# Moving a quarter of the conditioned weight deltas to GpSimd, with |h| written to a PSUM bank

## What is computed

```
scale = cond @ norm_w.T + 1.0
h = x * (scale[:, None, :] * rsqrt(mean(x * x) + EPS))
val, gate = split(h @ up_w.T)                  # 512 -> 2 x 2048
h = val * gelu(gate)
y = act_quant(h) @ weight_quant(down_w).T + x  # act_quant: one max |h| per row
# second layer, on y
dWd = ((h_lang @ Wdd.T + bdd) * 0.1).reshape(B, 128, 512)
dWu = ((h_lang @ Wdu.T + bdu) * 0.1).reshape(B, 512, 128)
out = y + relu(y @ (Wd + dWd) + bd) @ (Wu + dWu) + bu
```

## Time and profile before

| quantity | value |
|---|---|
| median of three runs | 942.75 us |
| the profiled execution | 943.0 us, its span 941.2 us |
| TensorE (PE) busy | 933.6 us, 99% |
| VectorE (DVE) busy | 675.3 us, 72% |
| ScalarE (ACT) busy | 437.6 us, 46% |
| GpSimd (POOL) busy | 53.4 us, 6% |
| granted TensorE clock | full in all 40 slices |

### The profile page before, as it was taken

One profiled execution on the slowest core, in us unless ns is written; L12 is line 12 of the kernel. 1 busy time (PEld: TensorE's weight loads), 2 busy tenths in 40 slices (PEclk: granted clock), 3 DMA queues, 4 the chain that ended last, 5 costly groups with the idle time before them and its releaser, 6 DMA issues.

```text
span 941.2 us, 13789 instructions
## 1 busy us (share of the span) xinstructions
PE 933.6 (99%) x5266; PEld 464.4 (49%) x5266; DVE 675.3 (72%) x1030; ACT 437.6 (46%) x800; POOL 53.4 (6%) x53
## 2 busy tenths in 40 slices
PE   8999999999999999999999999999999999999998
PEld 6555544444444444444444444444444444455586
DVE  5778888766877696767877687757877685256766
ACT  6898677224731276214742166213742255214443
POOL 1000000000000000000000000000000000000564
PEclk9999999999999999999999999999999999999999
DMA  8899654564346543664347543664347534421584
GB/s 286 239 219 217 169 151 131 150 193 137 101 140 170 161 134 112 159 168 155 112 131 177 152 138 99 173 174 146 110 127 186 149 90 135 112 68 35 185 307 179
DMA packets 118810, 145.36 MB, mean 154 GB/s; under 512 B 51796, under 2 KB 57432, under 8 KB 118232
## 3 DMA queue, kind: packets, MB, share of 16 engines
q1 hardware_dynamic: 118744, 144.48, 53.2%
HBM read 112.72 MB, written 20.97 MB: 142 GB/s over the span
## 4 chain that ended last, share of the span: by engine, by line
PE 97%; ACT 1%; DMA 1%; DVE 0%; issue 0%; SPq 0%; DVEq 0%; ACTq 0%
PE bank L1088 23%; PE bank L1090 23%; PE bank L1089 23%; PE bank L1190 10%; PE bank L1147 6%; PE bank L1200 1%; PE bank L1327 1%; PE bank L1336 1%; PE bank L1068 1%; PE bank L1349 1%; PE bank L1357 1%; PE bank L1359 1%; PE bank L1358 1%; PE bank L1366 1%; DMA xn<-in_x 1%; PE bank L1367 1%
## 5 line engine op out<-in xcount | busy, mean ns | idle before, releaser
L1088 PE MATMUL bank<-x_split,w_hi 128*128 128x512 f16 x1016 | 385.4, 379 | 0.0
L1089 PE MATMUL bank<-x_split,w_hi 128*128 128x512 f16 x1016 | 385.2, 379 | 0.0
L1090 PE MATMUL bank<-x_split,w_lo 128*128 128x512 f16 x1016 | 385.2, 379 | 0.0
L829 DVE STREAM_TRANSPOSE delta_reg<-delta_reg 128x512 f32<-128x512 f32 x256 | 262.4, 1108 | 51.7 <-DMA delta_reg<-in_L_cond_Wdu 19.3
L643 ACT ACTIVATE g<-h 128x512 f32<-128x512 f32 x128 | 80.6, 630 | 301.6 <-DVE h L925 301.6
L1090 PEld LDWEIGHTS bank<-x_split,w_lo 128*128 128x128 f16 x1016 | 99.4, 98 | 120.0
L1088 PEld LDWEIGHTS bank<-x_split,w_hi 128*128 128x128 f16 x1016 | 99.4, 98 | 119.2 <-issue 6.6
L1089 PEld LDWEIGHTS bank<-x_split,w_hi 128*128 128x128 f16 x1016 | 99.4, 98 | 113.2
L925 DVE SCALAR_TENSOR_TENSOR h<-bank,desc,g 128x512 f32<-128x512 f32 x128 | 93.1, 727 | 81.7 <-issue 57.9
L627 ACT ACTIVATE g<-bank,desc 128x512 f32<-128x512 f32 x128 | 87.5, 683 | 118.1 <-PE bank L1090 117.9
L1190 PE MATMUL bank<-wqT,qreg 128*128 128x512 fp8e4 x448 | 101.3, 379 | 0.0
(11 more groups left out here) (175 smaller groups left out, 628.6 us busy)
## 6 DMA issues: line engine op xcount, KB each, us to landing
delta_reg<-in_L_cond_Wdd SPq DMA_DIRECT2D x128, 256.0 KB, 2.9
delta_reg<-in_L_cond_Wdu SPq DMA_DIRECT2D x128, 256.0 KB, 2.9
qreg<-in_L_cond_up_w SPq DMA_DIRECT2D x32, 256.0 KB, 4.7
xr<-in_x SPq DMA_DIRECT2D x30, 256.0 KB, 3.8
x_scratch<-xr SPq DMA_DIRECT2D x30, 256.0 KB, 3.2
xn<-in_x SPq DMA_DIRECT2D x7, 1024.0 KB, 5.7
h<-in_L_cond_down_w SPq DMA_DIRECT2D x4, 1024.0 KB, 7.3
delta_reg<-in_L_cond_down_w SPq DMA_DIRECT2D x8, 512.0 KB, 4.6
```

The costliest lines, as they stand in the source:

```text
L829: dve.transpose(natT[:, t, k, :, :].rearrange("p a (r e) -> p e a r", e=4), nat[:, v % HALVES, :]).then_inc(nat_turned, 1)
L1088: pe.matmul(bank[:, :], w_hi[:, k, cols], xh[:, par, k, :], start=(k == 0), stop=False)
L1089: pe.matmul(bank[:, :], w_hi[:, k, cols], xl[:, par, k, :], start=False, stop=False)
L1090: mm = pe.matmul(bank[:, :], w_lo[:, k, cols], xh[:, par, k, :], start=False, stop=(k == KD - 1))
```

## The change

There are now 96 units on the old path, batched by four instead of eight, so that TensorE has 24 batches of 16 matmuls instead of 16 batches of 32 (a batch was 32 matmuls in the program, 64 in the trace, since each fp32 product is recorded twice). The remaining quarter of the delta rows, half of Wdu, is cut into 64 parts of 256 KB. SyncE loads a part into one of two places. GpSimd multiplies it by the four condition vectors (four instructions of 512 columns) and adds halves together twice (two of 512 and two of 256 columns), with waits on its own results between; VectorE sums the remaining 32 columns (`sum_part`, 64 of them, one in each slot of `sum_slots`) and later adds the result to the up weights (`up_weights`). GpSimd may be at most two parts ahead of VectorE's sums.

|h| is now written by ScalarE into the VAL bank that the value was in; VectorE's maximum reads it there, and TensorE's next value products into that bank wait for the maximum instead of for h. The scales are no longer copied by ScalarE to SBUF; VectorE multiplies by them out of PSUM bank TB. `s_bc` now holds the four condition vectors.

`load_deltas` now has 32 DMAs of 32 or 64 KB instead of 8 of 128 KB and 16 of 64 KB, and `turn_delta_up` has two transposes instead of four.

```diff
-    GROUPS = 16
-    UNITS, HALVES, NATT = 128, 3, 8
+    GROUPS = 12
+    UNITS, HALVES, NATT = 96, 3, 4
+    PARTS = 64
...
+        part_w = delta_reg[:, 11:13, :].rearrange("p s (d h) -> p s d h", d=4)
+        part_mul = delta_reg[:, 13:15, :].rearrange("p b (d h) -> p b d h", d=4)
+        part_low = delta_reg[:, 15:17, :].rearrange("p s (b d h) -> p s b d h", b=NB, d=4)
+        part_sum = delta_reg[:, 17:19, :].rearrange("p s e -> p (s e)").rearrange("p (b d) -> p b d", b=NB)
+        cond_all = s_bc[:, :].rearrange("p (b h) -> p b h", b=NB)
...
+        def abs_tile(c, j):
+            return g[:, j % 2, :] if is_last(c) and j >= FT - 2 else VAL[j % 2][:, :]
...
+        unit_slots, free_from = {}, 13
+        for n in range(FT * NCH):
+            long_slot = n >= FT and 9 <= n % FT < 13
+            while free_from <= n and sum(map(len, unit_slots.values())) < UNITS and len(unit_slots.get(n, [])) < 1 + long_slot:
+                u = sum(map(len, unit_slots.values()))
+                unit_slots.setdefault(n, []).append(u)
+                if u % NATT == NATT - 1:
+                    free_from = n + 2
+
         def units_at(c, j):
-            if is_first(c):
-                return [j - 13] if j >= 13 else []
-            if c == NCH - 1:
-                return [UNITS - 5 + j] if j < 5 else []
-            u = 3 + 20 * (c - 1) + j + min(max(j - 9, 0), 4)
-            return [u, u + 1] if 9 <= j < 13 else [u]
+            return unit_slots.get(FT * c + j, [])
 
         def batch_at(c, j):
-            before = units_at(c, j - 1) if j > 0 else units_at(c - 1, FT - 1) if c > 0 else []
-            return [m for u in before if u % NATT == NATT - 1 for m in (u // 4 - 1, u // 4)]
+            return [u // NATT for u in unit_slots.get(FT * c + j - 1, []) if u % NATT == NATT - 1]
+
+        def batch_of(m):
+            return (m % 2, m // 2) if m < 16 else (0, 8 + (m - 16) // 2 + 4 * (m % 2))
+
+
+        sum_slots = [FT * c + j for c in range(1, NCH)
+                     for j in ((7, 9, 10, 11, 12, 13, 15) if c == 1 else (1, 3, 5, 7, 8, 9, 10) if c == NCH - 1 else (1, 3, 5, 7, 9, 10, 11, 12, 13, 15))]
+        load_slots = [FT + 3, FT + 3, FT + 6] + [n + 1 for n in sum_slots[:PARTS - 3]]
+        assert len(sum_slots) == PARTS and len(load_slots) == PARTS
+
+        def parts_in(slots, n):
+            return [i for i, slot in enumerate(slots) if slot == n]
...
-                        sp.dma_start(delta_d[64 * k:64 * k + 64, b, :], delta_of[0, b, :, k, 0:4, :]).then_inc(delta_back, 16)
-                    for k in range(KD):
-                        part = delta_of[1, b, 32 * (k % 2):32 * (k % 2) + 32, k // 2, 0:4, :]
-                        sp.dma_start(delta_u[:, k, b, :], part).then_inc(delta_back, 16)
+                        n0 = 64 * k
+                        sp.dma_start(delta_d[n0:n0 + 32, b, :], delta_of[0][0, b, :, k, 0:4, :]).then_inc(delta_back, 16)
+                        for y in range(2):
+                            n1 = n0 + 32 + 16 * y
+                            sp.dma_start(delta_d[n1:n1 + 16, b, :], delta_of[1][y, b, :, k, 0:4, :]).then_inc(delta_back, 16)
+                        sp.dma_start(delta_u[:, 2 * k, b, :], delta_of[0][1, b, :, k, 0:4, :]).then_inc(delta_back, 16)
+
+            def load_part(i):
+                if i >= 2:
+                    sp.wait_ge(part_step, 8 * (i - 2) + 6)
+                d = 128 + 4 * i + 128 * (i // 32)
+                sp.dma_start(part_w[:, i % 2, :, :], Wdu.rearrange("(d n) h -> n d h", n=BN)[:, d:d + 4, :]).then_inc(part_in[i % 2], 16)
...
                     if first and j == 11:
+                        sp.wait_ge(ta_full, TA_BASE + 1)
+                        sp.dma_start(s_bc[:, :], cond.rearrange("(a b) c -> a (b c)", a=1).to_broadcast([P, CH])).then_inc(cond_all_in, 16)
                         for v in range(HALVES):
                             load_nat(v)
                     for u in units_at(c, j):
                         for v in (2 * u + HALVES, 2 * u + HALVES + 1):
                             if v < 2 * UNITS:
                                 load_nat(v)
+                    if c == 1 and j == 3:
+                        sp.wait_ge(piece_quant, FT)
+                    for i in parts_in(load_slots, FT * c + j):
+                        load_part(i)
...
+            def multiply_part(i):
+                pool.wait_ge(part_in[i % 2], 16 * (i // 2 + 1))
+                for pair in range(2):
+                    if i > 0 or pair > 0:
+                        pool.wait_ge(part_step, 8 * i + 4 * pair)
+                    for b in range(2):
+                        pool.tensor_tensor(part_mul[:, b, :, :], part_w[:, i % 2, :, :],
+                                           cond_all[:, 2 * pair + b, :].unsqueeze(1).to_broadcast([P, 4, C]), ALU.mult).then_inc(part_step, 1)
+                    pool.wait_ge(part_step, 8 * i + 4 * pair + 2)
+                    pool.tensor_tensor(part_mul[:, :, :, 0:64], part_mul[:, :, :, 0:64], part_mul[:, :, :, 64:128], ALU.add).then_inc(part_step, 1)
+                    pool.wait_ge(part_step, 8 * i + 4 * pair + 3)
+                    if i > 1 and pair == 0:
+                        pool.wait_ge(part_summed, i - 1)
+                    pool.tensor_tensor(part_low[:, i % 2, 2 * pair:2 * pair + 2, :, :], part_mul[:, :, :, 0:32], part_mul[:, :, :, 32:64],
+                                       ALU.add).then_inc(part_step, 1)
+
             def run(c, par, b):
-                if b is not None:
-                    norm_x(c + 1)
+                if is_first(c):
+                    norm_x(1)
+                    pool.wait_ge(cond_all_in, 16)
+
+                normed = is_first(c) or b is None
+                for i in range(PARTS):
+                    slot = sum_slots[max(i - 2, 0)]
+                    if slot // FT == c:
+                        if not normed and (i == 1 if c == 1 else slot % FT >= 6):
+                            norm_x(c + 1)
+                            normed = True
+                        multiply_part(i)
...
-            def copy_scales(c):
-                act.wait_ge(s_turned, c + 1)
-                act.activation(s_bc[:, :], TB[:, :], ACT.Copy).then_inc(s_bc_done, 1)
...
-                        act.wait_ge(max_done, n - 1)
+                        act.wait_ge(h_done, n - 1)
...
-                    act.activation(g[:, j % 2, :], h[:, j, :], ACT.Abs).then_inc(abs_done, 1)
+                    act.activation(abs_tile(c, j), h[:, j, :], ACT.Abs).then_inc(abs_done, 1)
...
-                    dve.wait_ge(s_bc_done, c + 1)
+                    dve.wait_ge(s_turned, c + 1)
 
                 for k in (k0, k0 + 1):
-                    dve.tensor_tensor(h[:, k, :], h[:, k, :], s_bc[:, :], ALU.mult).then_inc(h_scaled, 1)
+                    dve.tensor_tensor(h[:, k, :], h[:, k, :], TB[:, :], ALU.mult).then_inc(h_scaled, 1)
...
-                    dve.tensor_copy(absrun[:, :], g[:, 0, :]).then_inc(max_done, 1)
+                    dve.tensor_copy(absrun[:, :], abs_tile(c, 0)).then_inc(max_done, 1)
                 else:
                     dve.wait_ge(max_done, n)
-                    dve.tensor_tensor(absrun[:, :], absrun[:, :], g[:, j % 2, :], ALU.max).then_inc(max_done, 1)
+                    dve.tensor_tensor(absrun[:, :], abs_tile(c, j), absrun[:, :], ALU.max).then_inc(max_done, 1)
+
+            def sum_part(i):
+                dve.wait_ge(part_step, 8 * i + 8)
+                dve.tensor_reduce(part_sum[:, :, 4 * i:4 * i + 4], part_low[:, i % 2, :, :, :], AX.X, ALU.add).then_inc(part_summed, 1)
...
+            def up_weights(b, w, base_w):
+                dve.wait_ge(part_summed, PARTS)
+                dve.scalar_tensor_tensor(halves_of(w, 1), part_sum[:, b, :].rearrange("p (a d) -> p a d", a=2), DELTA_SCALE,
+                                         halves_of(base_w, 1), ALU.mult, ALU.add).then_inc(layers_wide, 1)
+                dve.scalar_tensor_tensor(halves_of(w, 0), halves_of(TB[:, :], 0), DELTA_SCALE,
+                                         halves_of(base_w, 0), ALU.mult, ALU.add).then_inc(layers_ready, 1)
...
+                    for i in parts_in(sum_slots, n):
+                        sum_part(i)
...
-                    pe.wait_ge(s_bc_done, NCH - 1)
+                    pe.wait_ge(h_scaled, FT * (NCH - 1))
                 else:
                     pe.wait_ge(layers_ready, 2 * b - 1)
                 for k in range(KD):
...
             def turn_delta_up(b):
                 if b > 0:
                     pe.wait_ge(layers_ready, 2 * b)
-                for k in range(KD):
+                for k in range(0, KD, 2):
...
-                        pe.wait_ge(h_done, n - 1)
+                        pe.wait_ge(max_done, n - 1)
...
```

(40 more changed lines are left out.)

18 lines of the change are left out of this document (11 added, 7 removed).

## The result

The kernel before ran at 941.95 us beside it (median of seven, 941.68 to 942.82), the changed one at 946.50 (median of seven, 944.20 to 948.92). The ratio is 1.0045, 95% interval 1.0033 to 1.0057: slower, by little but clear of the noise. The forecast was 942.0 and no measurable change. The profiled execution took 946.8 us, its span 944.6, against a forecast of 942.2.

The account below looks back on a forecast made before the run. TensorE, busy for 99% of the span, was taken as the bound. From the profiled 943.0 us, 13.7 and 0.9 come off, giving 928.4; 13.8 of waits in chunk 7 make 942.2, or 942.0 as a median; range 933 to 968.

Parts of the forecast that it names:

- likeliest case: The forecast itself, 942.0 us for the whole kernel, with its own range of 938 to 945; chance 0.47.
- second case: Rival: SyncE's delta DMAs in chunk 7 issue cheaper, TensorE only 6 us late, 934 us in all; chance 0.17.
- transposes: Eight fp32 transposes of the deltas leave TensorE in chunk 7: 0.9 us less.
- What leaves TensorE: Delta products: 16 batches of 3.69 us become 24 of 1.89, 13.7 us less; eight transposes go, 0.9 less.
- SyncE in chunk 7: Late delta DMAs and part 63 make TensorE wait about 6.5 and 7 us before the two down turns: 13.8 late.
- GpSimd's pace: A GpSimd part takes 9.7 us with gaps of 0.10; ten and one `rstd`, 98.5 us, fit a chunk of 104.2.
- GpSimd is the bound: Rival: self-waits of 0.25 us make a part 10.6 us, so h comes late; 962 to 999, taken as 975; chance 0.24.
- The shared port: Two-input VectorE instructions may hold up GpSimd by nothing to 5.7 us per chunk; half was taken, which fits.
- more than 0.75 us: Sign of a wrong prediction: VectorE instructions with two SBUF inputs show over 0.75 us or a wait in front.
- The lock alone: Rival: full port locks on both sides leave GpSimd no lead in long slots; 945 to 950 us; chance 0.12.
- |h| in PSUM: VectorE's maximum reading PSUM takes no longer, and TensorE's value products waiting for it cost nothing.
- The change does not do what it says: Rival: batches of half the size on TensorE could cost more than half; no size or chance of its own.

Follow-up runs that it names:

- e4: The kernel before with its 16 batches of delta products cut into 32 of half the size; 946.86 us, ratio 1.0046 to the kernel before.
- e3: The changed kernel with 115 idle products where TensorE waits for part 63 in chunk 7; 943.70 us, ratio 1.0012 to the kernel before.
- e1: The changed kernel with the load of part 63 issued ahead of the 32 delta DMAs; 937.24 us, ratio 0.9940 to the kernel before.
- e2: e1 plus a semaphore for each batch of delta DMAs and two xr loads moved ahead of the later three batches; 932.83 us, ratio 0.9898 to the kernel before.
- e6: The kernel before with |h| in the VAL bank and scales read from TB, no GpSimd work; 944.38 us, ratio 1.0019 to the kernel before.

## Why the prediction was wrong, step by step

The forecast was no measurable change and the likeliest case ended at 945; the kernel is slower, at 946.50. The wide range, to 968, takes it in only for the sake of cases that did not happen. (A small slip: all of the second case and four tenths of the first make 0.36, not 0.37.) In the profiled execution 946.8 stand against 942.2, 4.6 us more:

| step | predicted | measured |
|---|---|---|
| batches | -13.7 us | -10.2 |
| transposes | -0.9 | -0.9 |
| waits in chunk 7 | +13.8 | +11.1 |
| half clock behind the last wait | not in it | +2.5 |
| the rest, to make 946.8 | 0 | +1.3 |

- **What leaves TensorE: the step that failed.** I took a batch of half the records at half the time and said "the 0.09 of lead is all that the rows allow". It cost 1.96 and not 1.89, since a batch has 0.23 us of its own, and three batches waited 0.7 us for VectorE. The first is 24 x 0.07 = 1.7 us and the second 2.1; 0.3 come off, since the batches of before were that much longer than I had them. The earlier trace rows showed only one batch size, and a fixed cost can't be read from one size; e4 measured it. The waits were harder to see: of 12 batches whose fourth unit is turned in a slot that also quantises only three waited, one of them for a load. But the order of a slot on VectorE was known, and a bound above zero could have stood in the sum.
- **The clock is the term that was missing.** I priced a wait of 7 us at 7 us. It cost 9.8, because the clock fell during the wait and the work behind it ran at half clock for its first 5 us. e3 shows this alone, and e1 the two together. Every trace row of before had the full clock, so no row there priced it; the sum left the term out without saying so. With the 3.5 us of the batches these 2.5 are more than the whole 4.6 us.
- **SyncE in chunk 7: right in mechanism, place and releaser.** The last wait was forecast as about 7 us, released by VectorE behind the sum of part 63: 7.3, for that reason, and e1 removes it. The first was forecast as 6.4 and was 2.4, because the DMAs issued in 0.57 us, not 0.69; the 32 KB ones took 0.45, the price that I had as the lower end. The second was forecast as 0.4 and was 1.4: the `xr` load landed 5.1 us behind its issue, not 3.8. Part 63 was issued earlier than forecast on the same ground, but landed 5.4 us behind its issue, not 3.3, and TensorE too came earlier, which kept the last wait at its length. That 7.3 is so near to 7 is luck: errors of 2 to 4 us stand against each other.
- **GpSimd's pace: right.** In parts that nothing disturbs there are six gaps of 0.07 to 0.08 us, and a part takes 9.3 to 9.4 us, against 0.10 and 9.7. GpSimd is busy for 587 us more, against 590. `sum_part` waited for GpSimd three times in 64, 10.2 us, 9.4 of it for part 63. The rival "GpSimd is the bound" is out.
- **The shared port: real, and hidden.** L857 takes 1251 ns where its counterpart of before took 676, and L852 1060 where the row of before has 730. About 25 us of VectorE's time go there and 7 more in the small instructions below; GpSimd's multiplications stay at 1299 ns on average, near the 1293 of the additions in the earlier trace rows, with single ones up to 1727. The prediction named more than 0.75 us for such an instruction as a sign of being wrong, and the sign is there; but what it was to stand for, VectorE or GpSimd late at TensorE's cost, is not: before slot 10 of chunk 7 the only new waits of TensorE are the three of the batches, 1.9 us. The price on VectorE was the prediction's open term. The Trainium skill, page "SBUF — State Buffer", section "Who interferes with whom", states that an instruction of VectorE with two SBUF inputs and one of GpSimd that reads SBUF shut each other out: whichever starts first has the common ports for its whole length. The trace agrees: the longest L857 takes 1.09 us more than the shortest, less than one GpSimd multiplication, and the sum over 512 columns, which has one SBUF input, takes 615 to 722 ns. "The lock alone" named 945 to 950 and the time fell there, by luck and not by it: e2, with the same locks, is at 932.8.
- **|h| in PSUM: not at nothing.** I took the time out of PSUM from the maximum and overlooked its first step, the copy: 0.69 us and not 0.42. Alone the edit costs 1.8 us (e6); in the changed kernel an estimated 0.5 of the waits of the batches.
- **"The change does not do what it says"** was closest: part of the gain expected from the batches is never made. But it is 3.5 us of 13.7, not all.
- **Open:** of the last row of the table 0.4 us lie between TensorE's first transpose of chunk 7's maximum and the end: 79.5 us, against 79.1 before. The kernels with parts on GpSimd have 79.4 to 79.5 there, and those without (e4, e6) 79.2, so it goes with the parts. Another 0.4 lie around the span, and 0.5 were not found. I know the cause of none of them.

## What to carry to other kernels

Moving work to an idle engine cost the bounding engine little here while it ran, although VectorE paid 32 us for it, and a lot where it ended: find the last piece, and where its load stands in the DMA queue. Here one load placed behind 34 others was worth 9.3 us, twice the whole loss of the change. Price a long wait of TensorE above its own length (here 9.8 us for 7.3), because the clock may be lower behind it. And a group of half the size isn't half the cost: with only one size in the trace keep a fixed cost open in the sum.

## What the runs showed of the hardware that I had not expected

- TensorE's granted clock fell from 1.00 to 0.50 inside a gap of 7.3 us, between 826 and 827, and was still 0.50 for the first 5 us of work behind it; with idle products in the gap (e3) it stayed at 1.00, and that kernel was faster for the added work.
- Some of VectorE's 4-column instructions from SBUF to SBUF suffer beside GpSimd far more than their size says: L867 takes 554 ns on average, where the same one took 170 before; two others (L839, L863) 475 and 414 instead of 170. Others of that size (a reciprocal at 178, L868 at 219) don't change. What tells them apart no run here shows.
- A batch of the four-way split fp32 products takes 1.96 us for 32 records and 3.69 for 64 (e4), so half the size is more than half the time.
- A GpSimd instruction that waits for the one before it on its own engine starts 0.07 to 0.08 us behind its end, in the undisturbed parts of the changed kernel.
